# First token group of the expert stage prepared inside the first attention

## The chip, the cores and the metric

The kernel runs on one core of one Trainium2 chip. The metric is device time in microseconds (us) of one execution, and a kernel's figure is the median of its runs.

## What is computed

The reference takes `x` (4 sequences of 1024 tokens, width 256, so 4096 tokens) through four blocks, each added to `x`: a cross attention over 77 context rows, a mixture of experts, a second cross attention and a quantised MLP. The change lies between the first two:

```python
x = x + _L0_xattn_ref(ctx_1024, ctx_1024, _layernorm(x, axis=-1), mask_1x1xSxS2_fk1, ...)
x = x + _L0_ffn_ref(_layernorm(x, axis=-1), L0_ffn_router, L0_ffn_experts_gate, ...)

def _layernorm(x, axis=-1, eps=1e-05):
    m = jnp.mean(x, axis=axis, keepdims=True)
    v = jnp.var(x, axis=axis, keepdims=True)
    return (x - m) / jnp.sqrt(v + eps)
...
    router_probs = jax.nn.softmax(jnp.einsum('bsh,he->bse', x, router), axis=-1)
    topk_probs, topk_idx = jax.lax.top_k(router_probs, TOP_K)
```

Each token is normalised, the router (256 x 8) picks 2 of 8 experts for it, and a shared expert of twice the width runs on all tokens.

## The kernel before

The tokens stand as 32 tiles of 128 tokens (`T = 32`), 8 tiles to a sequence (`TB`). Five instruction streams are written by hand, one per engine, and meet in counted semaphores. Each phase is a block, and its end is a barrier of all engines.

**First attention** (`attention_phase`, layer 0). `lay_out_steps` writes out steps t = -4 to 32, and each step works on several tiles at different depths. On TensorE (`step` at L772) a step turns the probabilities of tile t, makes the queries of t + 2, turns the normalised rows of t + 3, projects the output of t - 1 (L762), makes the scores of t + 2 and weighs the values of t. VectorE masks the scores, takes row maxima, refines reciprocals (L911, L913), normalises the output to `ot` (L918), adds it to `x` (L923) and takes mean and variance (`stats` L927, `gather` L931). ScalarE takes exponentials (L821), copies turned tiles out of PSUM (L830), takes reciprocals by logarithm and exponential (L835, L837) and normalises tile t + 4 (L809). GpSimd subtracts the row maxima (L570, twice a step), adds the output bias (L576), forms the low halves of the expert weights in steps 8 to 22 (L580), and at three steps, called turns (-1, 8, 16), makes the normalising factors `rs` and `nm` of the attention's own normalisation for one sequence: `open_norm` (L142) at the end of that step and `close_norm` (L147, with a power of -0.5, L151) in the next. At step 32 only tile 31's last work is left: reciprocals, `ot`, projection, addition, statistics. TensorE closes with four filler matmuls (`keep_busy`).

SyncE fills the expert stage's slots in DRAM with zeros, 16 transfers whose source is the tile `sx[0]`, each let go by one finished tile.

**Expert stage** (`moe_phase`). Eight groups of four tiles (`NG = 8`, `ST = 4`). For a group, ScalarE normalises the rows into `sx` (L1367), TensorE turns them (`turn`, L1186), ScalarE copies the high part `xh` (L1373) and VectorE subtracts it to get the low part `xl` (L1506). Router, gate and up matmuls are then three products each of high and low parts (`three`, L1117 to L1119). `route` gives the logits, which ScalarE copies (L1378) and TensorE turns back (L1199); VectorE chooses the experts from them (`choose`, from L1515) and computes slot addresses; GpSimd scatters the rows to DRAM (L1161). The loop `group(s, u)` prepares group s + 1 while it computes group s. When all rows are scattered they are read back by expert, 40 half blocks in 20 steps, and computed with the experts' weights.

**The opening.** Group 0 has no group before it, so its preparation stands alone at the head of the block. VectorE adds epsilon to all variances (L116), ScalarE takes logarithm and exponential (L122, L124) and loads the table with SiLU (L1361), VectorE forms the factors for all 32 tiles (L131 to L139) and splits the router's weights into `wrh` and `wrl` (L1496 to L1500). Then come four normalisations, four turns into four PSUM banks (`first_bank`), four highs and four lows, and then `route(0, 0)`. TensorE fills the time ahead of its turns with six filler matmuls.

## Time and profile before

| | |
|---|---|
| median of 3 runs | 936.44 us (935.26 to 938.92) |
| the profiled execution | 939.79 us, span 938.1 us |
| TensorE matmuls busy | 824.9 us (88%) |
| VectorE busy | 740.2 us (79%) |
| ScalarE busy | 600.9 us (64%) |
| GpSimd busy | 534.5 us (57%) |
| mean granted TensorE clock | 0.958 |
| end of the first attention's last operation | 251.64 us after the span's start |

The span runs from the first to the last instruction of the profiled execution; its own time is 1.7 us longer, and stands 3.35 us above the median of the unprofiled runs. Times in the rows further down count from the span's start. PE is TensorE, PEld its weight loads, DVE VectorE, ACT ScalarE, POOL GpSimd. Busy shares are means over stages with different limits, so a single stage is read from windows and the timeline.

### The profile page before, as it was taken

What the parts mean: (1) busy time and instruction counts of PE and PEld (TensorE: products, weight loads), DVE (VectorE), ACT (ScalarE), POOL (GpSimd) and SP (SyncE); (2) the same over time, 40 slices, a digit from 0 to 9 for tenths busy, and PEclk for the clock granted to TensorE, in tenths of its full rate; (3) what the DMA queues carried; (4) which work ended last, traced back from release to release, by engine and by line L of the source; (5) the groups of instructions that cost most, each with busy time, mean ns of one, the idle gap of its engine ahead of it and who ended that gap; (6) DMA issues with size and microseconds to landing.
All of it is one profiled execution on the core that took longest, in us unless ns stands there. A gap on an engine that the chain in (4) does not pass through costs nothing. (4 is left out here: it accounts for less than half of the span.)

```text
span 938.1 us, 24346 instructions
## 1 busy us (share of the span) xinstructions
PE 824.9 (88%) x9260; PEld 669.3 (71%) x9260; DVE 740.2 (79%) x1661; ACT 600.9 (64%) x1106; POOL 534.5 (57%) x651
## 2 busy tenths in 40 slices
PE   5699999899688888799998599999998879999995
PEld 4588788788476767699998587777777645555563
DVE  3698888788557666578885888888889759999996
ACT  2466777666435443277873167777666759999994
POOL 2344767655124645347776598689988844443220
PEclk9799999999989999899999689999999989999997
DMA  8473799500001212356662845300303020004000
GB/s 262 72 292 126 265 384 392 230 3 2 1 30 67 86 64 90 98 169 204 216 196 100 305 99 85 47 3 2 47 2 46 2 35 23 23 29 85 23 29 28
DMA packets 55634, 100.04 MB, mean 107 GB/s; under 512 B 10208, under 2 KB 36448, under 8 KB 55520
## 3 DMA queue, kind: packets, MB, share of 16 engines
q1 hardware_dynamic: 38672, 70.12, 22.0%
q0 software_dynamic: 15232, 27.80, 11.7%
q8 instruction: 75, 1.23, 0.5%
q10 hardware_dynamic: 1616, 0.58, 0.3%
q14 instruction: 39, 0.32, 0.1%
HBM read 35.04 MB, written 59.24 MB: 101 GB/s over the span
## 5 line engine op out<-in xcount | busy, mean ns | idle before, releaser
L570 POOL TENSOR_TENSOR sm_a<-sm_a,mx_a 128x616 f32<-128x616 f32 x128 | 157.9, 1234 | 109.8 <-DVE mx_a L897 108.2
L821 ACT ACTIVATE pr_a<-sm_a 128x616 f32<-128x616 f32 x128 | 91.6, 715 | 85.2 <-POOL sm_a L570 85.2
L890 DVE TENSOR_TENSOR sm_a<-pS_a,mask 128x616 f32<-128x616 f32 x128 | 100.7, 791 | 23.3 <-PE pS_a L724 23.2
L1161 POOL DMA_INDIRECT slots<-sx,idx_f x64 | 65.0, 1016 | 81.4 <-DVE idx_f L1568 64.3
L1167 POOL DMA_INDIRECT mixed<-rep,qidx_f x80 | 78.2, 978 | 48.1 <-DVE rep L1677 24.7
L739 PE MATMUL pT_a<-ident,pr_a 128*128 128x128 f32 x640 | 97.8, 283 | 5.8 <-issue 2.4
L897 DVE TENSOR_REDUCE mx_a<-sm_a 128x8 f32<-128x616 f32 x128 | 99.0, 774 | 0.0
L762 PE MATMUL pO_a<-aw,ot_a 128*128 128x256 f32 x256 | 72.9, 408 | 23.9 <-DVE ot_a L918 23.2
L739 PEld LDWEIGHTS pT_a<-ident,pr_a 128*128 128x128 f32 x640 | 72.0, 143 | 20.9 <-issue 15.0
L713 PE MATMUL pA_a<-sx,aw 128*128 128x128 f32 x512 | 73.8, 291 | 0.5 <-ACT sx L815 0.5
L762 PEld LDWEIGHTS pO_a<-aw,ot_a 128*128 128x128 f32 x256 | 43.9, 191 | 42.4 <-DVE ot_a L918 39.0
L713 PEld LDWEIGHTS pA_a<-sx,aw 128*128 128x128 f32 x512 | 67.7, 206 | 1.5 <-ACT sx L815 1.2
L1846 PE MATMUL pU_m<-b,dg 128*128 128x512 f32 x128 | 61.9, 607 | 0.0
L724 PE MATMUL pS_a<-K,q_a 32*128 32x154 f32 x1024 | 54.1, 327 | 7.5 <-DVE q_a L903 7.0
L830 ACT ACTIVATE V<-pT_a 128x512 f32<-128x512 f32 (+1 forms) x96 | 46.5, 517 | 20.6 <-PE pT_a L739 20.5
L724 PEld LDWEIGHTS pS_a<-K,q_a 32*128 32x128 f32 x1024 | 38.7, 193 | 28.7 <-issue 19.0
L830 ACT ACTIVATE rep<-pT_a 128x512 f32<-128x512 f32 (+1 forms) x96 | 46.5, 517 | 14.0 <-PE pT_a L739 13.8
L754 PE MATMUL pO_a<-V 128*32 128x128 f32 x1024 | 52.7, 277 | 1.0 <-DVE x L923 1.0
L754 PE MATMUL pO_a<-rep,V 128*32 128x128 f32 x1024 | 52.2, 276 | 1.0 <-DVE x L923 1.0
L1805 POOL TENSOR_TENSOR se_m<-se_m,powers_m 128x1 f32<-128x1 f32 x32 | 17.9, 558 | 60.4 <-DVE se_m L1951 60.4
L754 PE MATMUL pO_a<-V,sel 128*32 128x128 f32 x1024 | 51.9, 273 | 0.1
L754 PE MATMUL pO_a<-rep,sel 128*32 128x128 f32 x1024 | 51.4, 273 | 0.0
(316 smaller groups left out, 2457.5 us busy)
## 6 DMA issues: line engine op xcount, KB each, us to landing
slots<-sx SPq DMA_DIRECT2D x16, 2176.0 KB, 9.3
sx<-slots SPq DMA_DIRECT2D x40, 272.0 KB, 3.2
x<-x_in SPq DMA_DIRECT2D x4, 1024.0 KB, 11.1
x<-mixed POOLq DMA_DIRECT2D x4, 1024.0 KB, 10.0
out_x<-x SPq DMA_DIRECT2D x32, 128.0 KB, 1.7
rep<-gu_in SPq DMA_DIRECT2D x10, 256.0 KB, 4.6
aw<-aw_in SPq DMA_DIRECT2D x2, 1024.0 KB, 6.9
ha<-mixed SPq DMA_DIRECT2D x2, 1024.0 KB, 7.2
```

What stands on the lines that cost most here:

```text
L570: pool.tensor_tensor(heads, heads, mx[u][:, g, :].rearrange("p (h a) -> p h a", a=1).broadcast_to([P, HG, SK]), ALU.subtract).then_inc(shi ...
L713: mm = pe.matmul(pA[:, D + g * P:D + (g + 1) * P], aw[:, k, g * P:(g + 1) * P], xt[u][:, k * P:(k + 1) * P], start=(k == 0), stop=(k == G ...
L724: mm = pe.matmul(pS[:, r, g * QS:(g + 1) * QS], q[u][own, g * P:(g + 1) * P], K[own, t // TB, g, :], start=True, stop=True, skip_group_che ...
L739: mm = pe.transpose(pT[:, (J * t + j) % 2, (n % 4) * P:(n % 4 + 1) * P], pr[u][:, g, c * P:(c + 1) * P], sb["ident"][:])
L754: mm = pe.matmul(pO[own, at:at + P], left, pt[u][:, g * CK + c, :], start=(g == 0 and r == 0 and what == 0), stop=(r == 1), skip_group_che ...
L762: mm = pe.matmul(pO[:, 0:D], ot[u][:, k * P:(k + 1) * P], aw[:, k, 3 * D:4 * D], start=(k == 0), stop=(k == G - 1), skip_group_check=True)
L821: act.activation(pr[u][:, g, 0:NS], sm[u][:, g, :], ACT.Exp).then_inc(exped, 1)
L830: act.activation(pt[u][:, lo:lo + n, :].rearrange("p n t -> p (n t)"), pT[:, (J * t + j) % 2, 0:n * P], ACT.Copy).then_inc(pt_sb, 1)
L890: dve.tensor_tensor(sm[u][:, g, :].rearrange("p (b h k) -> p b h k", b=ROWS_OF_HEADS, k=SK), pS[:, :, g * QS:(g + 1) * QS].rearrange("p b ...
L897: dve.tensor_reduce(mx[u][:, g, :], sm[u][:, g, :].rearrange("p (h k) -> p h k", k=SK), AX.X, ALU.max).then_inc(maxed, 1)
L1161: pool.indirect_dma_start(dram["slots"][:], bass.IndirectOffsetOnAxis(idx[:, at:at + 1], 0), rows[g % 2][:, j, :], None).then_inc(moved[g ...
L1167: pool.indirect_dma_start(dram["mixed"][:], bass.IndirectOffsetOnAxis(qidx[:, at:at + 1], 0), ys[q % 2][:, j, :], None).then_inc(out_moved ...
```

## The change

The preparation of group 0's four tiles moves into the first attention.

- Factors: GpSimd makes the expert stage's `rs` and `nm` inside the attention by four more turns: for tiles 0 to 7 at step 11, 8 to 15 at 19, 16 to 23 at 27 and 24 to 27 at 31. Only the last four tiles' factors are made at the head of the expert stage, by VectorE and ScalarE as before.
- ScalarE normalises tiles 0 to 3 into `sx[0]` at the ends of steps 28 to 31, with a wait for all zeroing transfers ahead of the first, and copies the four highs at step 32.
- TensorE turns the four tiles into the four banks of `pS` at step 32, ahead of the last projection. Its fillers there become six, into `pA`.
- VectorE splits the router's weights at the head of step 32, forms three lows ahead of the last addition, and the fourth between the last `stats` and `gather`.
- In the expert stage the opening on all engines goes, with TensorE's six fillers; semaphores are stepped to where it would have left them. `wrh`, `wrl` and the first of the `xh` and `xl` buffers are allocated ahead of the attention.

```diff
@@ attention_phase
+        own_norm, moe_norm, mlp_norm = ("rs", "nm", "queries"), ("rs", "nm", "experts"), ("rs_x", "nm_x")
         if layer == 0:
             turns = [(batch(b), -1 if b == 1 else TB * (b - 1), own_norm) for b in range(1, B)]
+            turns += [(batch(b), TB * (b + 1) + 3, moe_norm) for b in range(B - 1)]
+            turns += [(four(T // ST - 2), T - 1, moe_norm)]
+            turns.sort(key=lambda turn: turn[1])
...
+            turned_bank = lambda j: pS[:, j, 0:D].rearrange("p (k n) -> p k n", k=G)
...
+            def turn_first():
+
+                pe.wait_ge(masked, G * T)
+                for j in range(ST):
+                    pe.wait_ge(first_normed, j + 1)
+                    for k in range(G):
+                        mm = pe.transpose(pS[:, j, k * P:(k + 1) * P], sb["sx"][0][:, j, k * P:(k + 1) * P], sb["ident"][:])
+                    mm.then_inc(first_turned, 1)
...
+                if layer == 0 and t == T:
+                    turn_first()
                 if has(-1):
                     project(t - 1, 1 - u)
...
             if layer == 0:
-                pe.wait_ge(masked, G * T)
-                keep_busy(pe, sb, pS[:, 0, :], 4)
+                pe.wait_ge(q_sb, T)
+                keep_busy(pe, sb, pA, 6)
...
+            def norm_first(j):
+                if j == 0:
+                    act.wait_ge(sb["zeroed"], 16 * ZEROINGS)
+                act.wait_ge(factor_step, 4 * turned_by(j, moe_norm))
+                act.activation(sb["sx"][0][:, j, 0:D], X[:, j, :], ACT.Identity, scale=sb["rs"][:, j:j + 1],
+                               bias=sb["nm"][:, j:j + 1]).then_inc(first_normed, 1)
+
+            def high_first(j):
+                act.wait_ge(first_turned, j + 1)
+                act.activation(sb["xh_first"][opening(j)], turned_bank(j), ACT.Copy).then_inc(first_high, 1)
...
+            def low_first(j):
+                dve.wait_ge(first_high, j + 1)
+                dve.tensor_tensor(sb["xl_first"][opening(j)], turned_bank(j), sb["xh_first"][opening(j)].bitcast(F32),
+                                  ALU.subtract).then_inc(first_low, 1)
...
+                if layer == 0 and t == T:
+                    for j in range(ST - 1):
+                        low_first(j)
                 if has(-1):
                     add(t - 1)
...
@@ moe_phase
-            keep_busy(pe, sb, pGU[0][:, 0, :], 6)
-            for j in range(ST):
-                turn(0, 0, j, True)
-            pe.wait_ge(const_ok, 3)
             route(0, 0)
...
-            for j in range(ST):
-                norm(0, 0, j)
-            for j in range(ST):
-                x_high(0, 0, j, True)
             logits_out(0)
...
-            variance(dve, sb, slice(0, T), vr[:], variances)
+            variance(dve, sb, slice(T - ST, T), vr[:], variances)
...
-            for j in range(ST):
-                x_low(0, 0, j, True)
             choose(0, 0)
```

The order of VectorE's instructions at step 32 and at the head of the expert stage, before (the names are `ot_a` for the normalised output, `mv` for mean and variance, `lt_f` for the logits of a group):

```order
L911 TENSOR_TENSOR pO_a<-pO_a,rc_a 128x256
L913 SCALAR_TENSOR_TENSOR rc_a<-pO_a,rc_a 128x256
L918 SCALAR_TENSOR_TENSOR ot_a<-pO_a,rc_a 128x256
L923 TENSOR_TENSOR x<-pO_a,x 128x256
L927 BN_STATS st_a<-x 128x6
L931 BN_AGGR mv<-st_a 128x2
```

and with the change:

```order
L1037 MEMSET wrh 128x2x120
L1038 MEMSET wrl 128x2x120
L1039 CAST wrh<-rt 128x2x8
L1041 TENSOR_TENSOR wrl<-rt,wrh 128x2x8
L945 TENSOR_TENSOR pO_a<-pO_a,rc_a 128x256
L947 SCALAR_TENSOR_TENSOR rc_a<-pO_a,rc_a 128x256
L952 SCALAR_TENSOR_TENSOR ot_a<-pO_a,rc_a 128x256
L1045 TENSOR_TENSOR xl_first<-pS_a,xh_first 128x2x128 x3
L957 TENSOR_TENSOR x<-pO_a,x 128x256
L961 BN_STATS st_a<-x 128x6
L1045 TENSOR_TENSOR xl_first<-pS_a,xh_first 128x2x128
L965 BN_AGGR mv<-st_a 128x2
```

The split stands first, three lows stand ahead of the addition, and one ahead of the last gathering.

TensorE across the border of the two blocks, before (`pO_a` takes the projection, `pL_f` the router's logits):

```order
L762 MATMUL pO_a<-aw,ot_a 128x256 x2
L159 MATMUL pS_a<-ident 128x128 x4
L447 UNCONDITIONAL_BRANCH
L1173 UNCONDITIONAL_BRANCH
L159 MATMUL pGU_f<-ident 128x128 x6
L1186 MATMUL pX_f<-ident,sx 128x128 x2
L1186 MATMUL pGU_f<-ident,sx 128x128 x4
L1186 MATMUL pD_f<-ident,sx 128x128 x2
L1117 MATMUL pL_f<-xh_f,wrh_f 128x512
```

and with the change:

```order
L779 MATMUL pS_a<-ident,sx 128x128 x8
L769 MATMUL pO_a<-aw,ot_a 128x256 x2
L159 MATMUL pA_a<-ident 128x128 x6
L447 UNCONDITIONAL_BRANCH
L1228 UNCONDITIONAL_BRANCH
L1172 MATMUL pL_f<-xh_first,wrh 128x512
```

The eight turns stand ahead of the projection, and the router's first matmul is now the first of its block.

## Rows read from the trace of the kernel before

**Rows 1.** Window, attention: length; busy PE, PEld, DVE, ACT, POOL; clock; DMA; GB/s
```profile
200.00:210.00 10.00, 9.89 (x188) 8.13 (x189) 8.64 (x18) 6.65 (x14) 5.12 (x6) 1.00 0.01 2
```

**Rows 2.** Timeline, attention's end: start, us, engine, line, operation, idle before
```profile
235.01 0.38 ACT L835 ACTIVATE rc_a<-pO_a 128x256 f32<-128x256 f32 x1 [0.79 <-PE pO_a L754]
...
247.45 0.42 ACT L837 ACTIVATE rc_a<-rc_a 128x256 f32<-128x256 f32 x1
...
247.90 0.43 DVE L911 TENSOR_TENSOR pO_a<-pO_a,rc_a 128x256 f32<-128x256 f32 x1 [2.26 <-ACT rc_a L837]
...
248.89 0.42 DVE L918 SCALAR_TENSOR_TENSOR ot_a<-pO_a,rc_a 128x256 f32<-128x256 f32 x1
...
249.37 1.13 PE L762 MATMUL pO_a<-aw,ot_a 128*128 128x256 f32 x4 [2.41 <-DVE ot_a L918]
...
250.54 0.42 DVE L923 TENSOR_TENSOR x<-pO_a,x 128x256 f32<-128x256 f32 x1 [1.22 <-PE pO_a L762]
...
251.46 0.18 DVE L931 BATCH_NORM_AGGREGATE mv<-st_a 128x2 f32<-128x6 f32 x1
```

**Rows 3.** Timeline of the opening of the expert stage
```profile
252.43 1.58 PE L159 MATMUL pGU_f<-ident 128*128 128x128 f32 x12 [1.03 <-PEq L447]
...
253.53 1.28 ACT L1361 ACT_TABLE_LOAD   x1
...
254.83 2.08 ACT L1367 ACTIVATE sx<-x,nm,rs 128x256 f32<-128x256 f32 x4
...
257.60 0.38 ACT L1373 ACTIVATE xh_f<-pD_f 128x256 fp32r<-128x256 f32 x1
...
258.21 0.41 DVE L1506 TENSOR_TENSOR xl_f<-pD_f,xh_f 128x256 fp32r<-128x256 f32 x1
...
258.73 0.77 PE L1117 MATMUL pL_f<-xh_f,wrh_f 128*128 128x512 f32 x1 [1.33 <-issue]
...
261.66 0.60 ACT L1378 ACTIVATE lg_f<-pL_f 128x512 f32<-128x512 f32 x1 [3.68 <-PE pL_f L1119]
...
264.90 0.19 DVE L1515 COPY lt_f<-pL_f 128x32 f32<-128x32 f32 x1 [6.28 <-PE pL_f L1199]
```

**Rows 4.** Windows of that opening, columns as in rows 1
```profile
256.50:257.00 0.50, 0.45 (x3) 0.21 (x3) 0.00 (x0) 0.50 (x2) 0.00 (x0) 1.00 0.00 0
257.75:258.00 0.25, 0.00 (x0) 0.00 (x0) 0.25 (x2) 0.23 (x1) 0.00 (x0) 0.50 0.00 0
```

**Rows 5.** Timeline of the same stretch for group 1
```profile
276.58 0.40 PE L1117 MATMUL pL_f<-xh_f,wrh_f 128*128 128x512 f32 x1
...
278.17 0.60 ACT L1378 ACTIVATE lg_f<-pL_f 128x512 f32<-128x512 f32 x1 [3.26 <-PE pL_f L1119]
...
279.97 0.19 DVE L1515 COPY lt_f<-pL_f 128x32 f32<-128x32 f32 x1 [1.96 <-PE pL_f L1199]
```

**Rows 6.** Timeline of GpSimd, first row scatter of group 7
```profile
376.27 0.96 POOL L1161 DMA_INDIRECT slots<-sx,idx_f  x1 [2.21 <-DVE idx_f L1568]
```

**Rows 7.** Timeline of GpSimd around a turn of norm factors (steps 8 and 9)
```profile
93.42 1.22 POOL L570 TENSOR_TENSOR sm_a<-sm_a,mx_a 128x616 f32<-128x616 f32 x1 [1.65 <-DVE mx_a L897]
...
101.28 1.69 POOL L151 TENSOR_TENSOR rs<-var_a,powers_a 128x8 f32<-128x8 f32 x1
...
112.78 1.22 POOL L570 TENSOR_TENSOR sm_a<-sm_a,mx_a 128x616 f32<-128x616 f32 x1 [0.40 <-DVE mx_a L897]
...
119.23 1.22 POOL L570 TENSOR_TENSOR sm_a<-sm_a,mx_a 128x616 f32<-128x616 f32 x1 [0.40 <-DVE mx_a L897]
```

**Rows 8.** Timeline around a stall of TensorE
```profile
160.49 1.22 POOL L570 TENSOR_TENSOR sm_a<-sm_a,mx_a 128x616 f32<-128x616 f32 x1 [1.41 <-DVE mx_a L897]
...
172.81 1.22 POOL L570 TENSOR_TENSOR sm_a<-sm_a,mx_a 128x616 f32<-128x616 f32 x1 [1.38 <-DVE mx_a L897]
...
178.75 0.44 PE L739 MATMUL pT_a<-ident,pr_a 128*128 128x128 f32 x2 [2.45 <-issue]
...
189.13 1.22 POOL L570 TENSOR_TENSOR sm_a<-sm_a,mx_a 128x616 f32<-128x616 f32 x1 [1.39 <-DVE mx_a L897]
```

More of the change, by code:

```diff
@@ L859, in step @@
                     norm(t + 4, u)
+            def norm_first(j):
[7 more added lines that the diff above has]
+                act.activation(sb["xh_first"][opening(j)], turned_bank(j), ACT.Copy).then_inc(first_high, 1)
             def with_weights(t, u, has):
                 step(t, u, has)
+                if layer == 0 and T - ST <= t < T:
+                    norm_first(t - (T - ST))
+                if layer == 0 and t == T:
+                    for j in range(ST):
+                        high_first(j)
                 if layer == 1:
@@ L1012, in step @@
                     largest(t + 1, 1 - u, 1)
+                if layer == 0 and t == T:
+                    for j in range(ST - 1):
+                        low_first(j)
                 if has(-1):
@@ L1026, in step @@
                     mask(t + 2, u, 1)
+                if layer == 0 and t == T:
+                    low_first(ST - 1)
                 if has(-1):
@@ L1177, in _, with turn @@
             pe.sem_inc(q_down, 2)
-            def turn(g, u, j, opening=False):
+            def turn(g, u, j):
                 t = ST * g + j
                 pe.wait_ge(normed, t + 1)
-                to = first_bank[j] if opening else pX[:, 0:D]
-                if not opening:
-                    pe.wait_ge(xl_ok, t + 1)
+                pe.wait_ge(xl_ok, t + 1)
                 for k in range(G):
-                    mm = pe.transpose(to[:, k * P:(k + 1) * P], rows[u][:, j, k * P:(k + 1) * P], sb["ident"][:])
+                    mm = pe.transpose(pX[:, k * P:(k + 1) * P], rows[u][:, j, k * P:(k + 1) * P], sb["ident"][:])
                 mm.then_inc(xt_ps, 1)
```

49 lines of the change are left out of this document (29 added, 20 removed).

## The prediction

> **What bounds the kernel now.** I read the windows first. In the first attention TensorE is busy 9.89 of 10 us and VectorE 8.64 [rows 1], so that stage goes at the pace of a loop through TensorE and VectorE; ScalarE (6.65) and GpSimd (5.12) have room. The same row shows DMA traffic of 2 GB/s: the zeroing of the slots, which reads `sx[0]`, is long over by then.
>
> Then the timeline across the border of the two stages. The last tile's `x` is ready at 250.54 + 0.42 us, and its mean and variance end the attention at 251.64 [rows 2]. The next block begins at 252.43. From there a serial opening runs: variance, logarithm and exponential, an ACT table load, four normalisations, four turns, four high copies, four low differences, and only at 258.73 the first router matmul [rows 3]. Router logits leave PSUM at 261.66 and VectorE begins to choose experts at 264.90. Between 251.64 and 258.73 no engine does work that later groups need; every later group is chained to this one. That is the stretch to be shortened.
>
> Last the windows of that stretch: the granted clock is 1.00 (2.4 GHz) until 257.0 and 0.50 (1.2 GHz) from 257.75 [rows 4], behind a stretch in which TensorE had only the eight transposes of L1186, and gaps. So the router's matmuls run at the low clock. Group 1 shows the same stretch at full clock: from the first router matmul to the logits' copy 278.17 - 276.58 = 1.59 us, to VectorE's first step 279.97 - 276.58 = 3.39 us [rows 5]. In group 0 these are 261.66 - 258.73 = 2.93 and 264.90 - 258.73 = 6.17 us [rows 3].
>
> **The change, part by part.**
>
> *ScalarE, the four normalisations (steps 28 to 31).* They stand where the loop's own normalisation of tile t + 4 has run out. One takes 0.52 us (four in 2.08) [rows 3]; the idle time ahead of a late step's reciprocals is 0.79 us [rows 2]. Cost 0. If that cover were gone, 2.1 us would be on the loop.
>
> *TensorE, eight transposes before the last projection.* TensorE has 2.41 us idle there [rows 2]; each of the eight is a 128-column matmul, and the projection, four passes of twice the width, takes 1.13 [rows 2], so they need about as much. Cost 0.
>
> *ScalarE, four high copies of 0.38 us [rows 3].* They begin after the exponential ends at 247.87 [rows 2], and end by 247.87 + 4 x 0.38 = 249.4. ScalarE has nothing else until the next block. Cost 0.
>
> *VectorE.* The router split is four operations of 240 or 16 columns; at no more than the 0.43 us that 256 columns take they need 1.7 us, and the idle time ahead of the reciprocals' refinement is 2.26 [rows 2]. Three low differences of 0.41 us [rows 3] follow `ot` at 248.89 + 0.42 = 249.31 and end near 250.54, which is when the addition starts anyway because it waits for the projection ending at 250.50 [rows 2]. The fourth stands between statistics and their gathering: it puts the end of the attention off by at most 0.45 us, at least 0.1 if it fits the statistics' drain. I take **0.35 us**: the two neighbours are spaced so. Queued behind it is the block's end, which all engines wait for.
>
> *GpSimd, four turns of norm factors.* Each adds two small operations at a step's end and a power and a product at the next step's. The costliest is the power, 1.69 us [rows 7]. Steps 8 and 9 show such a turn today, in a step that also has the weight residues: from 93.42 to 112.78 are three steps, 19.36 us or 6.45 each, and the next, without a turn, takes 119.23 - 112.78 = 6.45 [rows 7]. So a turn costs the loop nothing; bounds 0 and 0.3 us each. Three turns (11, 19, 27) lie in the loop, the last (31) after its end. I take 0.
>
> *The wait for the zeroing on ScalarE (step 28).* Traffic is down at 200 us already [rows 1], step 28 comes near 229. Cost 0. No other DMA is moved, none is moved past on SP's or GpSimd's queue.
>
> *Expert stage: taken out.* Four normalisations, turns, highs, lows and the VectorE router split go. TensorE has nothing left ahead of the router matmuls but two increments by VectorE at its block's head. They start at 252.43 + 0.35, with a tenth for those increments: **252.9** instead of 258.73, 5.8 us earlier. Bounds 252.45 and 253.4.
>
> *Clock.* TensorE now has six filler matmuls after the projection, one gap of about 1 us, and then dense matmuls. In the trace of before the clock survived a thinner stretch (249.4 to 257.0). So I take the full clock, and group 1's durations: logits could be copied at 252.9 + 1.59 = 254.5.
>
> *What is late next: the ACT table.* It loads from 253.53 for 1.28 us [rows 3]; shifted by 0.35 it ends at 255.2. The copy takes 0.60, to 255.8. TensorE has finished its first gate half by then, and turns the logits back (0.6 us): VectorE's first step at about **256.5** instead of 264.90. The sum is **8.4 us**: 5.8 from the start, 2.8 from the clock (6.17 - 3.39), 0.2 lost to the table.
>
> The row also shows that nothing drains behind that load: the normalisation begins at 254.83, the load ends at 254.81 [rows 3]. The Trainium skill says otherwise ("ScalarE: Activation LUTs", What ACT_TABLE_LOAD costs): a switch of set takes a drain of some 1.38 us besides the load, by which the gain would be 7.0 us. I go by the row.
>
> *Does it arrive?* Group 7's row scatters start on VectorE's indices [rows 6], so the loads of the gathered rows, which wait for the scatters, move with the chain. Nothing in the program waits for a clock of its own. I carry 8.4 us to the end.
>
> **The sum.** The profiled execution took 939.79 us, 3.35 above the median of the runs shown; 939.8 - 8.4 = 931.4 for an execution like it, and 936.44 - 8.4 = **928.0 us** for the median.
>
> **Rivals.**
>
> *A, the half clock stays.* The eight added transposes are TensorE work that may not keep the clock up: in today's trace it fell behind just such eight. If it falls near 252, the router and first gate run at the low clock and take the 6.17 us of today: first step at 259.1, gain 5.8, **930.6 us**. Against it: the clock stood at 1.00 until 257.0, though TensorE had idled 2.41 us ahead of the last projection too [rows 2]. The Trainium skill ("TensorE: Matmul & The Clock Gate", Part 4: PE-mode transpose) has the rule behind it: transposes do not count as activity as other matmuls do.
>
> *B, the table holds ScalarE longer.* Today the next operation is let go by another engine; the new one, a copy out of PSUM under the new set, might be held. Priced as a second load, 1.28 us [rows 3], VectorE's first step comes at 257.8, gain 7.1: **929.3 us**. Against it, the normalisation 0.02 us behind the load. The Trainium skill's drain (above) is that mechanism.
>
> *C, part of the gain is lost on the way to an unrelated stall.* At 178.75 TensorE shows one: 2.45 us idle with no releaser, and the two steps around it take 189.13 - 172.81 = 16.32 us against 172.81 - 160.49 = 12.32 for the two before [rows 8], 4.0 us lost. The code after the border moves to other addresses and other times, so one such stall could appear: gain 4.4, **932.0 us**. Nothing in the trace places it.
>
> *D, slower: GpSimd's turns enter the loop.* The power stands between the two subtractions of the row maximum, and ScalarE's exponential, then TensorE's turns, wait for the second. If a turn holds TensorE back by its 2.4 us, the price is that of the stall, 4.0 us. Three turns cost 12.0, more than the 8.4 gained: 936.4 + 3.6 = **940.0 us**. It decides from 2.8 us a turn. Against it: the turn of steps 8 and 9 cost nothing [rows 7], though the steps from 16 on are shorter, 12.32 / 2 = 6.16 [rows 8], and leave less cover.
>
> **How the numbers follow.** Forecast 0.66; A 0.14; B 0.05; C 0.11; D 0.04. The low end: the lowest run, 935.26, with a gain of 8.4 and 0.5 more if the tail and start bounds fall well gives 926.4; another 0.9 if a later low-clock stretch is missed, 925.5. The high end takes in A, B and C: 932.5. D stays outside. A measurement of this kernel can tell about 0.5% from no change, 4.7 us: faster means under 931.8, slower over 941.1. Forecast, A and B lie under 931.8 nearly whole (0.81), C mostly above it, with the rest (0.16); D beyond 941.1 and unknown losses 0.03.
>
> **What would show it.** Right: eight transposes between 247 and 249 in the gap ahead of the last projection; attention's last operation near 252.0; first router matmul near 252.9 with a granted clock of 1.00; logits copy directly behind the table load at 255.2; VectorE's first step near 256.5; the same distance of about 8.4 us still there at the first loads of gathered rows and at the end. Wrong: steps 12, 20 or 28 longer than their neighbours (D); router matmuls at a granted clock of 0.50 (A); more than 1 us between load and copy (B); a distance that shrinks at one place with no releaser (C).

## The result, and the profile after

The changed kernel takes **929.42 us** (median of 6 runs, 927.11 to 933.82) against 935.85 us for the kernel before in the same session (6 runs, 932.26 to 938.92). The ratio is 0.9931, with a 95% interval of 0.9902 to 0.9959: 6.4 us less, between 3.8 and 9.2. The forecast was 928.0 with a range of 925.5 to 932.5. The whole interval lies below 1, its upper end nearer to 1 than the 0.5% that the prediction calls visible.

The profiled execution took 929.51 us. Its page, the span and the busy times:

```profile
span 927.8 us, 24350 instructions
...
PE 818.1 (88%) x9252; PEld 664.1 (72%) x9252; DVE 739.0 (80%) x1661; ACT 601.2 (65%) x1106; POOL 543.3 (59%) x667
...
```

TensorE's matmuls are busy 6.8 us less than the 824.9 of before and GpSimd is busy 8.8 us more, about what four turns hold (a power of 1.69 us [rows 7] and three small operations each). VectorE and ScalarE change by 1.2 us or less.

The timeline across the border of the stages, answering to [rows 2, 3] (start, duration, engine, line, operation, idle time before it with its releaser):

```profile
243.00 1.09 PE L779 MATMUL pS_a<-ident,sx 128*128 128x128 f32 x8
...
243.88 1.18 ACT L888 ACTIVATE xh_first<-pS_a 128x256 fp32r<-128x256 f32 x4
...
244.00 0.43 DVE L945 TENSOR_TENSOR pO_a<-pO_a,rc_a 128x256 f32<-128x256 f32 x1 [1.51 <-ACT rc_a L855]
...
245.34 1.08 DVE L1045 TENSOR_TENSOR xl_first<-pS_a,xh_first 128x256 fp32r<-128x256 f32 x3
...
245.48 1.13 PE L769 MATMUL pO_a<-aw,ot_a 128*128 128x256 f32 x4 [1.38 <-DVE ot_a L952]
...
246.44 1.50 PE L159 MATMUL pA_a<-ident 128*128 128x128 f32 x12
...
246.65 0.42 DVE L957 TENSOR_TENSOR x<-pO_a,x 128x256 f32<-128x256 f32 x1 [0.23 <-PE pO_a L769]
...
247.45 0.41 DVE L1045 TENSOR_TENSOR xl_first<-pS_a,xh_first 128x256 fp32r<-128x256 f32 x1
...
247.77 0.17 DVE L965 BATCH_NORM_AGGREGATE mv<-st_a 128x2 f32<-128x6 f32 x1
...
249.02 0.47 PE L1172 MATMUL pL_f<-xh_first,wrh 128*128 128x512 f32 x1 [1.08 <-DVEq L1527]
...
249.77 1.28 ACT L1413 ACT_TABLE_LOAD   x1
...
251.06 0.60 ACT L1430 ACTIVATE lg_f<-pL_f 128x512 f32<-128x512 f32 x1
...
252.47 0.19 DVE L1556 COPY lt_f<-pL_f 128x32 f32<-128x32 f32 x1 [1.64 <-PE pL_f L1253]
```

The reader sees the eight transposes begin at 243.00 and the four highs behind them, both done before the projection. Three lows follow `ot`, the addition waits only 0.23 us for the projection (1.22 in [rows 2]), and the fourth low lies between the statistics and their aggregation. The attention ends at 247.77 + 0.17 = 247.94, and the first router matmul starts **1.08 us** behind that, where it was 258.73 - 251.64 = 7.09 us. The table load ends at 249.77 + 1.28 = 251.05 and the copy of the logits begins at 251.06. VectorE's first step comes at 252.47, which is 4.53 us behind the attention's end, where it was 13.26.

The windows over the new border (length; busy PE, PEld, DVE, ACT, POOL; granted clock; DMA; GB/s), where before the clock read 0.50 [rows 4]:

```profile
246.00:248.00 2.00, 1.95 (x15) 1.69 (x13) 1.68 (x6) 0.00 (x0) 0.00 (x0) 1.00 0.00 0
...
250.00:251.00 1.00, 1.00 (x6) 0.82 (x5) 0.73 (x6) 1.00 (x1) 0.00 (x0) 1.00 0.00 0
```

The clock stays at 1.00 (2.4 GHz) through the fillers, the gap and the first gate half.

To compare two executions whose attention ends at different times, I count from a common point, the last refinement of reciprocals on VectorE (247.90 before [rows 2], 244.00 after):

| from that refinement to | before | after | gain |
|---|---|---|---|
| end of the attention | 3.74 | 3.94 | -0.20 |
| first router matmul | 10.83 | 5.02 | 5.81 |
| VectorE's first step | 17.00 | 8.47 | 8.53 |

The prediction's 8.4 us is there in this pair of profiles, and so are its places: on the time scale of the profile before, the router starts at 247.90 + 5.02 = 252.92 (252.9 was predicted) and VectorE's first step at 256.37 (256.5). But the spans differ by 938.1 - 927.8 = 10.3 us, and the medians by 6.4. Where these come apart was the question for the experiments.

Two things beside the opening differ in this pair. The profile after lacks the stall of [rows 8], 3.7 us of the difference by the time the attention ends. Further on, 12.6 us of distance at the last row scatter (385.44 against 372.83) shrink to 10.3 at the second attention's last operation (757.20 against 746.87). The larger part of that shrinking, 1.8 us, falls on the last tile there (the tile before it ends at 751.17 and 739.03, 12.1 apart), where the changed kernel's clock had fallen. Windows of the profile after there, columns as above:

```profile
738.00:740.00 2.00, 1.48 (x29) 1.32 (x32) 1.03 (x3) 0.26 (x1) 1.92 (x3) 0.65 0.14 21
...
740.00:742.00 2.00, 2.00 (x44) 1.64 (x36) 0.00 (x0) 0.00 (x0) 1.41 (x3) 0.50 1.19 171
```

The same stretch in a second profile of the changed kernel has 1.00 throughout, so this is not a consequence of the change in every execution.

### The profile page after: what moved, and what is told of

Its sections match the earlier page's. It is cut to its first block and busy times, and to the rows that moved or that the text cites. A ratio compares the mean times of both kernels' runs of the same rounds, so it can differ in the third digit from the quotient of the medians.

```text
span 927.8 us, 24350 instructions
## 1 busy us (share of the span) xinstructions
PE 818.1 (88%) x9252; PEld 664.1 (72%) x9252; DVE 739.0 (80%) x1661; ACT 601.2 (65%) x1106; POOL 543.3 (59%) x667
```

## The experiments

Kernels of one group below ran on one chip and share the runs of the kernel before. The groups ran on three chips. On the second and third the read-back of the expert stage takes 134 to 139 us instead of 102 in both kernels, so that the kernel before has 969.4 and 971.7 us there; times are compared inside a group only.

| kernel | time, us | ratio to before, 95% | attention's end to router | router to VectorE's first step |
|---|---|---|---|---|
| *group 1, before 934.23 (30 runs)* | | | | |
| after_again | 927.3 (7 runs) | 0.9927 (0.9901 to 0.9952) | 1.08 | 3.45 |
| before_again | 935.0 (12) | 1.0015 (0.999 to 1.0039) | 7.55 | 3.48 |
| hold_clock | 936.04 (12) | 1.0022 (0.9997 to 1.0047) | 8.35 | 3.48 |
| fewer_turns | 929.65 (12) | 0.9946 (0.9924 to 0.9969) | 1.08 | 3.48 |
| *group 2, before 969.41 (23 runs)* | | | | |
| turns_only | 972.97 (1) | | 7.08 | 6.17 |
| costly_turns | 968.29 (1) | | 1.08 | 3.45 |
| no_fillers | 966.71 (10) | 0.9978 (0.9953 to 1.0003) | 1.14 | 5.05 |
| table_early | 962.45 (12) | 0.9935 (0.9911 to 0.9959) | 1.09 | 3.47 |
| *group 3, before 971.7 (16 runs)* | | | | |
| before_third | 975.88 (1) | | 7.60 | 3.48 |
| split_late | 974.84 (1) | | 3.69 | 6.15 |
| turn_behind | 969.38 (1) | | 2.43 | 3.45 |
| moved_turn | 966.64 (11) | 0.994 (0.9916 to 0.9963) | 1.09 | 3.45 |

A single time scatters by several us (the 16 runs of before in group 3 lie between 969.28 and 978.07), so from the one-run rows only the profiles are read. Gains in us below are taken from the ratios.

### Both kernels again

after_again is the changed kernel as it stands.

> The changed kernel once more, for its spread and for a second profile. Theory (the opening of the expert stage is 8.5 us shorter and nothing else is changed; what the first profiles differ by elsewhere, a 4.0 us stall near 178 us and a low-clock stretch near 740 us, falls where it likes in each execution): the distance from the attention's last operation to VectorE's first step of group 0 is again 4.7 us (13.3 before), and at least one of the two other places looks different from the first profile; ratio to the kernel before 0.990 to 0.994. Rival (the change takes the stall away by itself, and moves the low-clock stretch): no stall and the same low clock at the end of the second attention again, ratio 0.989 or less.

The ratio, 0.9927, repeats the first one: a gain of 6.8 us. Its opening has 1.08 and 3.45 us, as in the first profile. A stall of the kind of [rows 8] has come back, by the timeline:

```profile
177.10 0.56 PE L746 MATMUL pT_a<-ident,pr_a 128*128 128x128 f32 x2 [2.44 <-issue]
```

So its absence from the first profile of the changed kernel was no effect that the change always brings, and the 3.7 us in the difference of those two spans do not belong to the opening.

before_again is the kernel before as it stands.

> The kernel before once more, as a control of the measurement. Theory: ratio 1.000 within its interval, VectorE's first step of group 0 again 13.3 us behind the attention's end; the 4.0 us stall near 178 us absent or elsewhere. Rival (the stall belongs to this program): the stall is there again at the same instruction.

The time is the same (1.0015). The stall of [rows 8] is there again, at 177.56 with 2.45 us, as the rival had it. The opening is not the same: 11.03 us from the attention's end to VectorE's first step, where the theory had 13.3. Its timeline, with the last refinement, the attention's closing fillers and end, the first router matmul and VectorE's first step:

```profile
246.65 0.43 DVE L911 TENSOR_TENSOR pO_a<-pO_a,rc_a 128x256 f32<-128x256 f32 x1 [2.26 <-ACT rc_a L837]
...
249.09 1.80 PE L159 MATMUL pS_a<-ident 128*128 128x128 f32 x8
...
250.22 0.18 DVE L931 BATCH_NORM_AGGREGATE mv<-st_a 128x2 f32<-128x6 f32 x1
...
257.95 0.47 PE L1117 MATMUL pL_f<-xh_f,wrh_f 128*128 128x512 f32 x1 [1.33 <-issue]
...
261.43 0.19 DVE L1515 COPY lt_f<-pL_f 128x32 f32<-128x32 f32 x1 [3.58 <-PE pL_f L1199]
```

The router matmul is 0.47 us long, as at full clock, where [rows 3] have 0.77 for the same line. From it to the first step are 3.48 us, where [rows 3] have 6.17. The windows say why:

```profile
250.00:251.00 1.00, 0.90 (x5) 0.60 (x3) 0.36 (x2) 0.00 (x0) 0.00 (x0) 0.50 0.00 0
...
256.00:257.00 1.00, 0.62 (x4) 0.20 (x2) 0.57 (x2) 1.00 (x5) 0.00 (x0) 0.98 0.00 0
```

Here the clock fell *earlier*, behind TensorE's idle 2.41 us ahead of the last projection: the window of 249 to 250 reads 0.60, those from 250 to 256 read 0.50 (1.2 GHz), and it is back for the last of the transposes and the router. The closing fillers of the attention take 1.80 us, where the first profile has the same work at full clock:

```profile
250.34 1.05 PE L159 MATMUL pS_a<-ident 128*128 128x128 f32 x8
```

So they end at 250.89, 0.49 us behind VectorE's last operation, and the border between the blocks waits for them: the router comes 7.55 us behind the attention's end instead of 7.09. In the first profile the clock fell behind the transposes and lay on the router [rows 4]. Counted from the refinement, the first step comes at 261.43 - 246.65 = 14.78 us, where the first profile has 17.00. So the prediction's clock term, 2.8 us, is a property of an execution, not of the kernel before.

hold_clock tests the term itself: the kernel before with enough filler matmuls that the clock can't fall.

```diff
-            keep_busy(pe, sb, pGU[0][:, 0, :], 6)
+            keep_busy(pe, sb, pGU[0][:, 0, :], 20)
             for j in range(ST):
                 turn(0, 0, j, True)
+            keep_busy(pe, sb, pGU[0][:, 0, :], 10)
             pe.wait_ge(const_ok, 3)
             route(0, 0)
```

> The kernel before with 14 more filler matmuls at the head of the expert stage and 10 between the turns and the router: the opening stays, the clock should not fall. Theory (2.8 of the 8.5 us are the clock's): granted clock 1.00 from 252 to 265 us of the old time scale, the router's first matmul where it was or up to 0.3 us later, VectorE's first step 2.5 to 2.8 us nearer to the attention's end, total 2.5 us less, ratio 0.997. Rival (the clock was no part, all came from the start): VectorE's first step moves by under 1 us.

Timeline and one window:

```profile
257.19 0.48 PE L1117 MATMUL pL_f<-xh_f,wrh_f 128*128 128x512 f32 x1
...
260.67 0.19 DVE L1516 COPY lt_f<-pL_f 128x32 f32<-128x32 f32 x1 [4.26 <-PE pL_f L1199]
...
254.00:256.00 2.00, 2.00 (x20) 2.00 (x20) 1.01 (x4) 1.31 (x5) 0.00 (x0) 1.00 0.00 0
```

The clock was held: 1.00 in that window and through the router, and 3.48 us to the first step. But the fillers stand on the chain themselves. The router came 8.35 us behind the attention's end (248.84 to 257.19) instead of 7.1 to 7.6, the whole opening took 11.83 us against 11.03 in before_again, and the time is unchanged, 1.0022, where the theory had 2.5 us less with a router at most 0.3 us later. The high clock alone is worth nothing here if it has to be bought with TensorE work ahead of the router.

### The four turns on GpSimd

turns_only adds the four turns of norm factors to the kernel before, and nothing uses their results; the change's other parts are left out.

```diff
...
+            turns += [(batch(b), TB * (b + 1) + 3, moe_norm) for b in range(B - 1)]
+            turns += [(four(T // ST - 2), T - 1, moe_norm)]
+            turns.sort(key=lambda turn: turn[1])
```

> The kernel before with GpSimd's four new turns alone; their factors are overwritten at the head of the expert stage, where all stays as it was. Theory (a turn is free while steps last 6.45 us, and costs about 0.3 us once they last 6.16): steps around 12 keep 6.45 us, those around 20 and 28 are 0.1 to 0.3 us longer once, 0.4 to 0.6 us in all. Rival (turns are free everywhere): no step differs. The opening, from the attention's end to VectorE's first step of group 0, is a third sample of the clock: 13.3 us with the fall inside it, 11.0 without.

The pair of steps around step 12 took 12.90 us, twice the 6.45 of [rows 7]; around step 20 it was 0.25 us longer than its neighbours; around 28 it took 12.32, twice the 6.16 of [rows 8]. That is 0.25 us in all, under the 0.4 to 0.6 expected. The attention's end to the first step took 13.25 us in this profile, the low clock on the router again. The same is to be seen in the changed kernel. GpSimd's first subtraction of rows, its timeline, two steps apart around steps 12 and 28:

```profile
115.39 1.22 POOL L577 TENSOR_TENSOR sm_a<-sm_a,mx_a 128x616 f32<-128x616 f32 x1 [1.68 <-DVE mx_a L931]
...
128.28 1.22 POOL L577 TENSOR_TENSOR sm_a<-sm_a,mx_a 128x616 f32<-128x616 f32 x1 [1.68 <-DVE mx_a L931]
...
215.96 1.22 POOL L577 TENSOR_TENSOR sm_a<-sm_a,mx_a 128x616 f32<-128x616 f32 x1 [1.38 <-DVE mx_a L931]
...
228.36 1.22 POOL L577 TENSOR_TENSOR sm_a<-sm_a,mx_a 128x616 f32<-128x616 f32 x1 [1.47 <-DVE mx_a L931]
```

128.28 - 115.39 = 12.89 us is free, 228.36 - 215.96 = 12.40 is 0.08 more than 12.32. With 0.27 around step 20 (no_fillers shows it without a stall beside it: 12.59 us) the turns cost **about 0.35 us**, where the prediction took 0. The fourth, at step 31, costs nothing: from GpSimd's last subtraction to the last refinement are 9.81 us with it (234.19 to 244.00) and 9.82 without (238.08 to 247.90). The pair around step 12 is not free in every execution. It took 13.14 to 13.15 us in the profiles of fewer_turns, table_early and moved_turn, 0.25 more, and no run here says why.

costly_turns shows how near to the edge that is: each new turn gets two more powers, of 1.67 us, into scratch tiles.

```diff
...
+                        if to == moe_norm:
+                            pool.wait_ge(factor_step, 4 * n + 2)
+                            for m in range(2):
+                                pool.tensor_tensor(burned[2 * n + m][:, 0:wide], vr[n][:, 0:wide], powers[:, 0:wide], ALU.pow)
```

> The changed kernel with two more powers (1.67 us each) in each of the four new turns, so that three turns inside the loop hold GpSimd 3.3 us longer. Theory (a step's second subtraction has about 2 us of cover at most, and the loop pays what exceeds it): the three steps grow by 2.5 to 3.5 us each, the attention ends 7 to 10 us later, and the total is at or above the kernel before. Rival (GpSimd is so far from the loop that even this is covered): under 1 us a turn.

Around step 28, the same rows of GpSimd:

```profile
221.40 1.22 POOL L578 TENSOR_TENSOR sm_a<-sm_a,mx_a 128x616 f32<-128x616 f32 x1 [1.39 <-DVE mx_a L936]
...
236.97 1.22 POOL L578 TENSOR_TENSOR sm_a<-sm_a,mx_a 128x616 f32<-128x616 f32 x1 [2.67 <-DVE mx_a L936]
```

236.97 - 221.40 = 15.57 us, where the plain turn has 12.40: of the added 3.34 us of GpSimd work 3.17 come through. Around step 20 it is 3.22 (15.81 against 12.59), around 12 it is 2.91 (15.80 against 12.89). So a turn leaves 0.1 to 0.2 us of cover where steps take 6.16 us, and 0.4 us where they take 6.45. GpSimd's low busy share in [rows 1] is no room: its work is on the chain inside a step. Rival D's mechanism is real. Only its size was missing in the changed kernel. The expectation had the total at or above the kernel before; the one run took 968.29 us against a median of 969.41, and one run can't tell.

fewer_turns keeps one of the four turns (step 11) and has VectorE and ScalarE make the factors of tiles 8 to 31 at the head of the expert stage.

```diff
-            turns += [(batch(b), TB * (b + 1) + 3, moe_norm) for b in range(B - 1)]
-            turns += [(four(T // ST - 2), T - 1, moe_norm)]
+            turns += [(batch(0), TB + 3, moe_norm)]
...
-                if t == T - ST:
+                if t == TB:
                     act.wait_ge(factor_step, 5)
...
-            variance(dve, sb, slice(T - ST, T), vr[:], variances)
+            variance(dve, sb, slice(TB, T), vr[:], variances)
```

> The changed kernel with only the first of GpSimd's four new turns (step 11); the factors of tiles 8 to 31 are made at the head of the expert stage by VectorE and ScalarE, as 24 columns in place of 4. Theory (a turn costs the attention nothing): the steps around 19 and 27 keep their period, attention ends at most 0.2 us earlier, same total as the changed kernel within 0.5 us in the profile. Rival (turns enter the loop where steps are 6.16 us long): the attention ends 0.3 us a turn, 0.6 us or more, earlier.

The two steps around step 20 took 179.47 - 167.15 = 12.32 us again, and so did those around 28: 0.27 + 0.08 = 0.35 us less, between the theory's 0.2 and the rival's 0.6. The opening stayed at 1.08 + 3.48 us. The ratio, 0.9946, can't be told from 0.9927. Three of the four turns are therefore not what the gain rests on: they cost some tenths, and nothing that they save is seen.

moved_turn moves one turn away from the weight residues that GpSimd forms until step 22, from step 19 to 23.

```diff
-            turns += [(batch(b), TB * (b + 1) + 3, moe_norm) for b in range(B - 1)]
+            turns += [(batch(b), (11, 23, 27)[b], moe_norm) for b in range(B - 1)]
```

> The changed kernel with the turn of tiles 8 to 15 at step 23 in place of 19, behind the last weight residue. Theory (a turn costs 0.27 us where GpSimd also has a residue in the step and steps last 6.16 us, nothing elsewhere): steps around 20 and 24 keep 6.16 us, attention's two steps around 20 take 12.32 us in place of 12.59; the total is within noise of the changed kernel. Rival (the cost is the turn's own, wherever it stands): 0.27 us shows at step 24 instead.

Around steps 20 and 24, GpSimd's timeline:

```profile
164.48 1.22 POOL L577 TENSOR_TENSOR sm_a<-sm_a,mx_a 128x616 f32<-128x616 f32 x1 [0.40 <-DVE mx_a L931]
...
176.79 1.21 POOL L577 TENSOR_TENSOR sm_a<-sm_a,mx_a 128x616 f32<-128x616 f32 x1 [0.40 <-DVE mx_a L931]
...
199.29 1.22 POOL L577 TENSOR_TENSOR sm_a<-sm_a,mx_a 128x616 f32<-128x616 f32 x1 [0.99 <-DVE mx_a L931]
...
211.68 1.22 POOL L577 TENSOR_TENSOR sm_a<-sm_a,mx_a 128x616 f32<-128x616 f32 x1 [1.64 <-DVE mx_a L931]
```

176.79 - 164.48 = 12.31 us without the turn, and 211.68 - 199.29 = 12.39 with it, 0.07 more than 12.32. The 0.27 us of step 20 is the turn *and* a weight residue in one step. Moving it gives back 0.2 us, which no time here can show (0.994).

### Fillers, table, split and the place of the turns

no_fillers takes the six filler matmuls at the attention's end out of the changed kernel.

```diff
                 pe.wait_ge(q_sb, T)
-                keep_busy(pe, sb, pA, 6)
```

> The changed kernel without the six filler matmuls behind the last projection. Theory (the clock in the new opening does not hang on them, since the gap ahead of the router is then 2.3 us, no longer than the idle times that the trace shows at 1.00): first router matmul at the same distance from the attention's end (1.1 us), granted clock 1.00, VectorE's first step 4.5 us behind the end, same total. Rival A (the fillers hold the clock): granted clock 0.50 for the router and the first gate, VectorE's first step 7.3 us behind the end, total 2.8 us more.

Timeline and windows over the border:

```profile
248.12 0.47 PE L1171 MATMUL pL_f<-xh_first,wrh 128*128 128x512 f32 x1 [2.47 <-DVEq L1526]
...
253.17 0.19 DVE L1555 COPY lt_f<-pL_f 128x32 f32<-128x32 f32 x1 [3.30 <-PE pL_f L1252]
```

```profile
246.00:248.00 2.00, 0.00 (x0) 0.00 (x0) 0.94 (x4) 0.00 (x0) 0.00 (x0) 1.00 0.00 0
...
248.00:249.00 1.00, 0.89 (x4) 0.78 (x5) 0.58 (x5) 0.60 (x3) 0.00 (x0) 1.00 0.00 0
...
250.00:251.00 1.00, 1.00 (x4) 0.81 (x3) 0.00 (x0) 0.97 (x3) 0.00 (x0) 0.50 0.00 0
```

The router starts as in the changed kernel, 1.14 us behind the attention's end (246.98 to 248.12), and its first matmul still takes 0.47 us. But the first window shows TensorE with no matmul for 2 us, and from inside the router on the granted clock is low: 0.50 at 250. From the router matmul to the first step are 253.17 - 248.12 = 5.05 us instead of 3.45. That is **1.6 us** that the fillers save in this profile. The theory on record, the same clock without them, was wrong, and the rival's first step at 7.3 us behind the attention's end is here at 6.19. The prediction's rival A named the transposes as the reason, and the Trainium skill ("TensorE: Matmul & The Clock Gate", Part 4: PE-mode transpose) says that a transpose doesn't count as TensorE being busy in the same way. No run here parts that from the gap of 2.47 us ahead of the router, which could do it alone. The whole time, 966.71, is 4.3 us above table_early's of the same group. The profile can't account for that: it is of the fastest of the ten runs, 960.98 us. Of the 4.3, 1.6 may be the opening; the rest has no place.

table_early loads the SiLU table at the attention's end, and GpSimd makes the last four factors at the head of the expert stage, since the logarithm is no longer loaded.

```diff
                     for j in range(ST):
                         high_first(j)
+                    act.preload_act_table_set("silu_and_others")
...
-            inverse_root(act, vr[:], yr[:], 0, variances, roots)
-            act.preload_act_table_set("silu_and_others")
```

> The changed kernel with the SiLU table loaded at the end of the attention, behind the last high copy, and the last four tiles' factors made by GpSimd at the head of the expert stage; VectorE's and ScalarE's chain of variance, logarithm and exponential goes. Theory (the table load ends just as the logits are ready and costs 0.1 us at most): VectorE's first step 4.4 to 4.5 us behind the attention's end in place of 4.53, total within noise of the changed kernel. Rival (the load holds back the copy behind it): 0.5 us or more nearer.

The rows of the logits' copy and of VectorE's first step:

```profile
249.99 0.60 ACT L1433 ACTIVATE lg_f<-pL_f 128x512 f32<-128x512 f32 x1 [4.32 <-PE pL_f L1175]
...
251.81 0.19 DVE L1557 COPY lt_f<-pL_f 128x32 f32<-128x32 f32 x1 [2.82 <-PE pL_f L1258]
```

The copy comes 1.65 us behind the router matmul (248.34) instead of 251.06 - 249.02 = 2.04, so the load in its old place did hold it by 0.4 us. But the first step comes 3.47 us behind the router matmul and 4.56 behind the attention's end, as before. The load was not on the path. The expected rival (the load holds back the copy, and VectorE's step with it) is out, and so is the prediction's rival B: in the changed kernel the copy starts 0.01 us behind the load (251.05, 251.06). The Trainium skill ("ScalarE: Activation LUTs", What ACT_TABLE_LOAD costs) has a drain of some 1.38 us besides the load, and neither these two rows nor [rows 3] show one.

before_third is the kernel before again, on the third chip.

> The kernel before, for one more sample of its opening. So far the distance from the attention's end to VectorE's first step of group 0 was 13.3, 11.0 and (with GpSimd's turns alone) 13.3 us. Theory (the clock falls inside the opening in some executions and costs 2.7 us there): one of these two values again. Rival (it varies over the whole width between): a third value.

It took 11.08 us from the attention's end to the first step, with the clock at 0.50 from 250 to past 256.5 and 1.00 from 257, the form of before_again. So of four profiles with the old opening two have the low clock on the router (13.26 and 13.25 us) and two ahead of it (11.03 and 11.08). hold_clock, whose fillers hold it up, is not counted.

split_late puts the split of the router's weights back to the head of the expert stage.

```diff
@@ first attention, VectorE
-                if layer == 0 and t == T:
-                    split_router()
@@ expert stage, VectorE, behind the factors
...
+            dve.tensor_copy(wrh[:, :, 0:NE], sb["rt"][:]).then_inc(const_ok, 1)
+            dve.wait_ge(const_ok, 2)
+            dve.tensor_tensor(wrl[:, :, 0:NE], sb["rt"][:], f32(wrh[:, :, 0:NE]), ALU.subtract).then_inc(const_ok, 1)
@@ TensorE
+            pe.wait_ge(const_ok, 3)
             route(0, 0)
```

> The changed kernel with the router's split put back behind VectorE's factors at the head of the expert stage, and TensorE waiting for it. Theory (the router waits for whatever is left in front of it): the split ends 2.5 us after VectorE's first operation there, so the router's first matmul is 3.4 to 3.7 us behind the attention's end in place of 1.1, and VectorE's first step of the group 6.9 to 7.2 in place of 4.5 (up to 9.9 if the clock falls in the longer gap). Rival (the table load sets the pace anyway): first step under 1 us later.

Timeline, and windows over the border:

```profile
256.20 0.80 PE L1170 MATMUL pL_f<-xh_first,wrh 128*128 128x512 f32 x1 [3.69 <-DVE wrl L1547]
...
262.35 0.19 DVE L1561 COPY lt_f<-pL_f 128x32 f32<-128x32 f32 x1 [6.21 <-PE pL_f L1251]
```

```profile
252.00:254.00 2.00, 0.51 (x5) 0.32 (x3) 0.83 (x7) 0.12 (x1) 0.00 (x0) 1.00 0.00 0
...
256.00:258.00 2.00, 1.80 (x4) 1.49 (x5) 0.15 (x1) 0.00 (x0) 0.00 (x0) 0.50 0.00 0
```

TensorE waits 3.69 us for four small operations of VectorE that stand behind the chain of factors, and in that time the clock falls: 1.00, then 0.50. VectorE's first step comes 9.84 us behind the attention's end (252.51) instead of 4.53. That is 2.6 us for the wait and 2.7 for the clock, against the 4.53. A part of the change that costs under 1 us of VectorE's work carries 5.3 us in this profile.

turn_behind sets the eight transposes behind the last projection and all four lows behind the last aggregation.

```diff
-                if layer == 0 and t == T:
-                    turn_first()
                 if has(-1):
                     project(t - 1, 1 - u)
+                if layer == 0 and t == T:
+                    turn_first()
...
-                if layer == 0 and t == T:
-                    for j in range(ST - 1):
-                        low_first(j)
...
-                if layer == 0 and t == T:
-                    low_first(ST - 1)
                 if has(-1):
                     gather(t - 1, 1 - u)
+                if layer == 0 and t == T:
+                    for j in range(ST):
+                        low_first(j)
```

> The changed kernel with the eight transposes behind the last projection and all four lows behind the last gathering. Theory (the place ahead of the projection is free, behind it is not): the lows follow the statistics, the attention's last operation comes 1.0 to 1.5 us later than with the changed order (its last low ends 6.9 to 7.4 us behind the first of the last reciprocals' two refinements in place of 3.9), everything behind it keeps its distances, 1.1 and 4.5 us. Rival (transposes take the place of fillers, so no loss): under 0.3 us later.

The expectation gives two numbers that don't fit each other: 1.0 to 1.5 us later, and 6.9 to 7.4 us in place of 3.9, which is 3.0 us or more. Counted from the refinement, by the timeline and the windows:

```profile
247.51 0.43 DVE L945 TENSOR_TENSOR pO_a<-pO_a,rc_a 128x256 f32<-128x256 f32 x1 [1.51 <-ACT rc_a L855]
...
248.98 1.13 PE L769 MATMUL pO_a<-aw,ot_a 128*128 128x256 f32 x4 [2.41 <-DVE ot_a L952]
...
249.95 1.76 PE L779 MATMUL pS_a<-ident,sx 128*128 128x128 f32 x8
...
251.17 1.42 DVE L1045 TENSOR_TENSOR xl_first<-pS_a,xh_first 128x256 fp32r<-128x256 f32 x4
...
251.50 2.46 PE L159 MATMUL pA_a<-ident 128*128 128x128 f32 x12
...
255.02 0.47 PE L1170 MATMUL pL_f<-xh_first,wrh 128*128 128x512 f32 x1 [1.05 <-DVEq L1525]
```

```profile
248.00:250.00 2.00, 1.02 (x5) 0.87 (x6) 0.82 (x2) 0.00 (x0) 0.00 (x0) 1.00 0.00 0
...
251.00:252.00 1.00, 1.00 (x7) 1.00 (x6) 0.96 (x5) 0.92 (x3) 0.00 (x0) 0.50 0.00 0
```

The router comes at 255.02 - 247.51 = 7.51 us where the changed kernel has 5.02: **2.5 us** later. Two things make it up. The four lows stand in a row on the chain and end at 251.17 + 1.42 = 252.59; with the 1.08 us of the border the router would come 6.2 us behind the refinement, 1.1 later. The last low ends 5.08 us behind the refinement, 1.1 later than the changed kernel's last operation, which is the first of the expected numbers; the second was wrong. But TensorE idles the old 2.41 us ahead of the projection again, and this time the clock reads 0.50 behind it. The fillers take 2.46 us instead of 1.50 and end at 253.96, and the router follows 1.06 us behind *them*. So the distances behind the attention's end did not keep: 2.43 us to the router in place of 1.1. The other 1.4 us are transposes (1.76 us against 1.09) and fillers at the low clock, at a border that waits for all engines. How much of it belongs to the order is open: of the six profiles that leave 2.41 us idle ahead of the last projection, the clock fell behind it in three (this one, before_again, before_third) and stayed at 1.00 there in three (before, turns_only, hold_clock). With the transposes in it the gap is 1.38 us, and the clock stayed at 1.00 behind the projection in all eight profiles.

## Why the prediction was right

The forecast's case came about, and its chain was the right one. By its own steps:

- **Start of the router.** Predicted 5.8 us earlier, measured 5.81 against the same profile. Against before_again it is 11.30 - 5.02 = 6.3, since the closing fillers ran at the low clock there and held the border by 0.5 us.
- **The fourth low.** Predicted 0.35 us, measured 0.20. The first router matmul stands 1.08 us behind the attention's end, where the text's numbers make 0.9.
- **Cover at nothing.** Normalisations, transposes and highs cost nothing that shows: projection and `ot` keep their places, and the addition still begins 2.65 us behind the refinement (246.65 - 244.00; 250.54 - 247.90 = 2.64 before). The idle times they were laid into were real.
- **The clock, 2.8 us.** This is the term that was mis-sized. The prediction read the low clock on the router in one profile and took it for a fixed cost. It was there in two profiles of four (6.17 us from router to first step) and lay ahead of the router in two (3.48), where it cost some 0.5 us through the attention's closing fillers. Over the four, router to first step averages 4.8 us against 3.45: a term of 1.4 us in place of 2.8. From the attention's end to the first step the four have 13.26, 13.25, 11.03 and 11.08 us, mean 12.15, against 4.53.
- **The table, 0.2 us lost.** Nothing that shows is lost. The copy comes behind the load, at 251.06, some 0.4 us later than 249.02 + 1.59 would allow, but VectorE waits for TensorE, whose turning back of the logits stands behind the first gate half (the first step's releaser is `pL_f`), and table_early gains nothing.
- **The turns, 0.** Measured 0.35 us over all four, inside the bounds of 0 to 0.3 each.
- **Does it arrive?** It does, in both forms of the old opening. From the attention's end to the last row scatter are 133.80 us (before) and 131.53 (before_again), against 124.89 and 124.85 with the change: 8.9 and 6.7 us less, of which the opening has 8.7 and 6.5.

The sum with these sizes: 12.15 - 4.53 = 7.6, less 0.2 for the low and 0.35 for the turns, makes **7.1 us**. Measured are 6.4 (3.8 to 9.2) and 6.8 us, where 8.4 was predicted. The first measurement fell 2.0 us short of the forecast gain, and the re-sized terms give 1.3 of that; the intervals alone could not tell 7.1 from 8.4, and four profiles are few for a mean. The time itself came nearer, 929.42 against 928.0, by some luck: the forecast started from 936.44, and the kernel before had a median of 935.85 in the later session, which hides 0.6 us of the missing gain.

**The rivals.** A (the half clock on the router and the first gate) did not happen in any of the seven profiles that keep the fillers and the early split. It did in the one profile each where either was taken out, with 1.6 and 2.7 us. B did not happen: the load held the copy by 0.4 us, and table_early shows that VectorE's step does not depend on it. D did not happen at the turns' own size, 0.35 us over all four against the 2.8 us each from which it would decide; costly_turns shows that its mechanism is real, and that some 2.8 us more of GpSimd work a turn would, by its rows, have used up the gain. C, the stall, is the one left open. Stalls of TensorE of 2.2 to 2.7 us with no releaser stand between 177 and 180 us in all five profiles with the old opening and in four of the nine with the new. In eight of these nine the steps around it lose 3.7 to 4.2 us, and the granted clock falls to 0.50 for some 3 us behind it; in hold_clock, where the clock stayed at 1.00, they lose 2.1 us, the stall's own 2.17. So about half of the 4.0 us that the prediction read from [rows 8] goes with the clock. Nothing that I ran moves it on purpose, the measured gains fit without it, and so few profiles don't show that the change affects it.

**What each part is worth.** From the single-part kernels, one profile each: moving the split ahead 5.3 us, the transposes in the gap ahead of the projection and the lows ahead of the addition 2.5, the fillers 1.6. In each, about half or more is the clock, or TensorE work at the low clock (2.7, 1.4 and 1.6), and since the place of its fall differs between executions, these parts are single draws. What does not hang on the clock is 2.6 us for the split and 1.1 for the order. The parts overlap and don't add. Three of the four turns are worth nothing that is seen. No kernel here was faster than the changed one by more than its measurement can tell.

## What to carry to other kernels

Where one block ends in a dependent tail and the next begins with a serial head, look for the tail's idle times and place the head's work into them operation by operation; each has its own gap. An operation placed behind the tail instead (as in turn_behind) is on the chain again. Work in TensorE's gap went along with a held clock here (eight profiles of eight, against three of six with the gap left idle), but that is a count, not a proof. Before pricing a low clock as a gain, take more than one profile: where it falls can differ between executions of the same kernel, and its cost with it. An engine that is half idle has no room if its work stands inside the loop's chain; add a few us there, as costly_turns does, to see what the cover is.

## What the runs showed of the hardware that I had not expected

- The granted clock fell at two different places in executions of one kernel: behind the attention's last projection (0.60 at 249 to 250, then 0.50 to 256) or behind the opening's transposes, over its router (0.50 at 257.75). The same opening took 11.03 and 11.08 us with the early fall, 13.26 and 13.25 with the late one.
- With six filler matmuls, 1.50 us, ahead of a 1.08 us gap the clock stayed at 1.00 in all six profiles that have both; without them the gap was 2.47 us, the clock fell to 0.50 and 1.6 us were lost. In split_late a gap of 3.69 us did the same, and cost 2.7. Fillers that run at the low clock are themselves waited for at a block's border: 2.46 us in turn_behind, and 1.80 in place of 1.05 in before_again.
- Forcing the clock up with fillers on the chain (hold_clock) cost as much as it gave: 11.83 us against 11.03 to 13.26.
- TensorE's stalls near 175 to 180 us come and go between executions of the same kernel (absent in the first profile of the changed kernel, 2.44 us in the second). Eight of nine cost 3.7 to 4.2 us, more than half of the change's whole effect, with the clock at 0.50 behind them; the ninth, with the clock at 1.00, cost 2.1. A difference of two single spans (10.3 us here) is therefore no measure of a change of this size (6.4).
- The same program spends 102 us on one chip and 134 to 139 on two others in reading back the scattered rows, with the same work in it, and the change's gain is about the same there: 6.3 us (4.0 to 8.6) in table_early, 5.8 (3.6 to 8.2) in moved_turn.
